# Rounded parts for two chunks of an output product, and a plain mean as the bias of the squares

## The chip, the cores and the metric

The kernel runs on one core of one Trainium2 chip. The metric is device time in microseconds, from launch to the last store. The engines of a core run at the same time and wait for each other on semaphores: TensorE (PE, with its weight loads as PEld), VectorE (DVE), ScalarE (ACT), GpSimd (POOL), and SyncE (SP), which issues the transfers.

## What is computed

One transformer block on 16 sequences of 1024 rows of 512 numbers, in float32: attention over 32 learned patterns with sparsemax in place of softmax, a residual and a normalization, then a small feed-forward part with a residual and a second normalization.

```python
A   = sparsemax((x @ Wq + bq).reshape(B, L, 16, 32) . keys / sqrt(32))
out = einsum('bhls,bshd->blhd', A, values)
out = transpose(out, (0, 2, 1, 3)).reshape(B, L, 512) @ Wo + bo
x   = layernorm(x + out)
s   = einsum('btd,dm->btm', x, Win) + bin_
h   = relu(s[..., None] * W1 + b1)
g   = einsum('btmh,mh->btm', h, W2) + b2
x   = layernorm(x + einsum('btm,md->btd', g, Wout) + bout)
```

The transpose ahead of the reshape mixes heads into rows, so that one row of `out @ Wo` belongs to one head and gathers 16 neighbouring rows of `A`. The kernel folds values and `Wo` into one matrix G for each head (512 by 512, four chunks of 128 rows). The "output product" of a tile is then four products of 128 by 128 probabilities with a 128 by 512 chunk of G.

## The kernel before, in words

The 16384 rows are 128 tiles of 128 rows. The order of the work is written out by hand as 151 slots. In slot n every engine does, for each step of the pipeline, that step for tile n minus the step's lag (the `LAG_` numbers): transposes of x in slot n for tile n, scores one slot later, the sparsemax steps up to lag 9 or 10, the output product at lag 23 (`LAG_WO`), the first normalization at lags 24 and 25, the feed-forward part at 26 to 34, the second normalization at 35 and 36. Each engine works through its own list in order, so an instruction that waits holds back all that is behind it on its engine.

**Start.** Slots 0 to 22 have no output product. In slots 5 to 20 the matrix G is made, one unit a slot (`pieces`, `piece`): a unit is four heads (index a) of one chunk c, so unit n has c = n mod 4 and lies in slot n + 5. PE multiplies (L891), ACT copies the four results from PSUM into four rows of a staging buffer, which are rows of `y_sb` (L1114), at the end of its slot, and SP stores them in four transfers to `G_of_heads` in DRAM (L454). There are two staging buffers, used in turn; the copies of a unit wait until the unit two slots before is stored. In the slots before 23 POOL also subtracts the step from the scores (L613), and in every slot up to 129 it folds two sums for the sparsemax (`fold`, L566), after ACT has written `side` and `above` (L1088, L1090). Within ACT's slot the order is: count (L1045), rounding of the transposed x (`xT_hi`, L1075, which waits for the score of the tile before, since there is one `xT_hi`), probabilities (L976, in two slots out of four), `side`, `above`, probabilities again, and then the copies of G.

**Output product.** SP loads the 1 MB of G of a head from DRAM for every tile (L467), into a ring of two. PE runs four float32 products (L856), each of which is issued as two matrix instructions. The scores of a tile are computed otherwise (`three_pass`, L749 to L751): each float32 operand is split into a rounded part and the rest, both of the type float32r, and hi times hi, hi times lo and lo times hi are added up, one instruction each.

**Normalization.** DVE adds the residual and sums the row (L1269). POOL makes two numbers of the sum, the mean scaled by the root of the row's length (L541) and the plain mean (L543). ACT squares with the first one as bias (L989). POOL makes the reciprocal root and the shift (L551, L556, L559), and ACT applies them (L1059, L1053). Every fourth slot ("split slot" below) has extra work: ACT and POOL add up and split the feed-forward sum (L1033, L1068, L1069 on ACT, L595 and L597 on POOL).

One tile of the first twelve needs a full sort on DVE, which takes DVE from 91 to 118 us.

Of the kernel before, what the change touches and what calls it, by code (L numbers as in the profile page):

```python
# [49 lines left out]
LAG_G = 22  # L50
# [14 lines left out]
def build_kernel(nc, query, key_param, Wq, bq, Wk, bk, Wv, bv, Wo, bo,  # L65
# [23 lines left out]
    with ExitStack() as ctx:  # L89
# [9 lines left out]
        GR, STAGES = 2, 2  # L99
# [26 lines left out]
        pT = sb("pT", [P, 2 * H * C * P])  # L126
        sum1 = sb("sum1", [P, 2])
        minus_mean1 = sb("minus_mean1", [P, 2])
        shift_sq1 = sb("shift_sq1", [P, 2])
# [13 lines left out]
        shift_sq2 = sb("shift_sq2", [P, 2])  # L143
# [8 lines left out]
        G_sb = sb("G_sb", [P, GR, C, D])  # L152
        V_rep, VT_rep = G_sb[:, 0].rearrange("p c n -> p (c n)"), G_sb[:, 1, 0, :]
        G_dram = nc.dram_tensor("G_of_heads", [H, P, C * D], F32, kind="Internal").ap()
# [18 lines left out]
        eps = sb("eps", [P, 1])  # L173
        per_row = sb("per_row", [P, 1])
        per_row_sq = sb("per_row_sq", [P, 1])
# [46 lines left out]
        s_Gst = [sem(f"s_Gst{r}") for r in range(STAGES)]  # L222
# [132 lines left out]
        def pair_place(turn, i):  # L355

            return (turn + i // UNROLL) % 2 * (H * C * P)
# [34 lines left out]

        def group_of(turn, i):

            return turn * (UNROLL // GROUP) + i // GROUP
# [3 lines left out]
        FILLS = 14 + S  # L399
# [3 lines left out]
        def _(sp):  # L403
# [35 lines left out]

            def slot(turn, j):  # L440
# [5 lines left out]
                for k in pieces(turn, j - 2):  # L446
                    heads, c, a = piece(k)
                    if a < HPC - 1:
                        continue
                    r = k // HPC % STAGES  # L450
                    sp.wait_ge(s_Gev, k + 1)
                    for n in range(HPC):
                        places = G_dram[HPC * heads + n].rearrange("(a s) n -> s a n", s=S)
                        sp.dma_start(places[:, :, c * D:(c + 1) * D],  # L454
                                     y_sb[n * S:(n + 1) * S, r * HPC:(r + 1) * HPC, :]).then_inc(s_Gst[r], 16)
                if in_range(turn, j, LAG_G):
                    i = j - LAG_G
                    h = i % H
                    if isinstance(turn, int) and base + i < H:
                        if h == 0:  # L460
                            sp.wait_ge(s_Gmm, PIECES)
                        if h % HPC == 0:
                            for r in range(STAGES):
                                sp.wait_ge(s_Gst[r], 16 * HPC * (h // HPC + 1) * (C // STAGES))
                    if not isinstance(turn, int) or base + i >= GR:
                        sp.wait_ge(s_o, base + i - GR + 1)
                    sp.dma_start(G_sb[:, i % GR].rearrange("p c n -> p (c n)"), G_dram[h]).then_inc(  # L467
                        s_G[i % GR], 16)
                if in_range(turn, j, LAG_XB):
                    i = j - LAG_XB  # L470
                    if base + i == 0:
                        for r in range(STAGES):
                            sp.wait_ge(s_Gst[r], 16 * (PIECES // STAGES))
# [32 lines left out]
        def _(pool):  # L506
# [15 lines left out]
            nc.gpsimd.memset(eps[:], EPS).then_inc(s_const, 1)  # L522
            nc.gpsimd.memset(per_row[:], -1.0 / D).then_inc(s_const, 1)
            nc.gpsimd.memset(per_row_sq[:], -1.0 / D ** 1.5).then_inc(s_const, 1)
# [11 lines left out]
            def mean(t0, par, s_rows, total, s_mean, minus_mean, shift_sq, s_shift):  # L536
# [9 lines left out]
            def norm(t0, par, s_var, var, s_ve, ve, s_mean, minus_mean, s_rstd, rstd, s_shift, shift, s_used):  # L546
# [4 lines left out]
                nc.gpsimd.tensor_tensor(ve[:], var[:, par:par + 1], eps[:], ALU.add).then_inc(s_ve, 1)  # L551
# [5 lines left out]
                pool.wait_ge(s_mean, 2 * t0)  # L557
# [11 lines left out]
            def slot(turn, j):  # L569
# [22 lines left out]
                if lead is not None and lead < ON_VECTOR:  # L592
# [6 lines left out]
                    pool.wait_ge(s_lo, lead // GROUP + 1)  # L599
                if in_range(turn, j, LAG_NORM1):  # L600
                    i = j - LAG_NORM1
                    mean(base + i + 1, i % 2, s_r1, sum1, s_mean1, minus_mean1, shift_sq1, s_shift1)
                if in_range(turn, j, LAG_NORM2):
                    i = j - LAG_NORM2
                    mean(base + i + 1, i % 2, s_r2, sum2, s_mean2, minus_mean2, shift_sq2, s_shift2)
# [9 lines left out]
                if in_range(turn, j, LAG_SIDE):  # L615
                    i = j - LAG_SIDE
                    fold(s_side, base + i + 1, side, s_foldc)
                    fold(s_above, base + i + 1, above, s_folds)

# [35 lines left out]
            mean(TILES, (TILES - 1) % 2, s_r1, sum1, s_mean1, minus_mean1, shift_sq1, s_shift1)  # L655
# [26 lines left out]
        def _(pe):  # L682
# [61 lines left out]
            def three_pass(ps, hi, lo, w_hi, w_lo, start, first):  # L744

                for c in range(C):
# [4 lines left out]
                    mm = nc.tensor.matmul(ps[:], lo[:, c, :], w_hi[:, c, :], start=False, stop=(c == C - 1))  # L751
                return mm
# [65 lines left out]
            def slot(turn, j):  # L818
# [26 lines left out]
                if in_range(turn, j, LAG_WO):  # L845
# [6 lines left out]
                    pe.wait_ge(s_G[i % GR], 16 * (turns_of(turn, j, LAG_WO, GR) + 1))  # L852
                    if not isinstance(turn, int) or base + i >= 2:
                        pe.wait_ge(s_r1, base + i - 1)
                    for c in range(C):
                        mm = nc.tensor.matmul(o_ps[i % 2][:],  # L856
                                              pT[:, bass.ds(pair_place(turn, i) + (i % H * C + c) * P, P)],
                                              G_sb[:, i % GR, c, :], start=(c == 0), stop=(c == C - 1))
                    mm.then_inc(s_o, 1)
# [22 lines left out]
                for k in pieces(turn, j):  # L882
# [3 lines left out]
                    if k >= HPC:  # L886
                        pe.wait_ge(s_Gev, k - HPC + 1)
# [655 lines left out]
```

## Time and profile before

| what | value |
|---|---|
| median of three runs | 1311.17 us (1311.08 to 1311.61) |
| profiled execution | 1313.41 us, of which span 1311.6 us |
| PE busy | 1248.0 us (95%) |
| DVE, ACT, POOL busy | 1133.2 us (86%), 1068.2 us (81%), 676.5 us (52%) |
| bytes moved by DMA | 258.35 MB, mean 197 GB/s |

The busy time is a mean over three stages: the start up to the first output product at 184 us, a long middle to 1141 us in which every slot holds all steps, and an end in which no scores are left. Matrix instructions are pipelined and overlap in the records, so the time that one takes is read from its start to the start of the next.

### The profile page before, as it was taken

The numbers are of one execution on the slowest core, as the hardware profiler recorded it, in microseconds if no ns is written. First come the engines' busy times: TensorE is split into PE (matmuls) and PEld (weight loads), VectorE is DVE, ScalarE is ACT, GpSimd is POOL, SyncE is SP. The second block draws the span as 40 slices with busy tenths as digits, with TensorE's granted clock in tenths as the row PEclk, the third lists the DMA queues.
The fourth block names the chain that finished last, engine by engine and source line by source line (L and its number), as shares of the span: only waits on it lengthen the run. The fifth ranks groups of instructions, "written<-read, shape, count | busy, mean of one in ns | idle before, by whom it ended". The sixth has DMA issues, their size and how long they took to land. (4 is left out here: it accounts for less than half of the span.)

```text
span 1311.6 us, 25223 instructions
## 1 busy us (share of the span) xinstructions
PE 1248.0 (95%) x5848; PEld 853.4 (65%) x5848; DVE 1133.2 (86%) x4538; ACT 1068.2 (81%) x2285; POOL 676.5 (52%) x1634
## 2 busy tenths in 40 slices
PE   8973899999999999999999999999999999989995
PEld 5642566676766767676776767677676767655552
DVE  3986899899999999999999999999999999966776
ACT  3661865779898888989898888989898888987776
POOL 1431333346555555655565555656555555665654
PEclk9995999999999999999999999999999999999998
DMA  6480785655656556565656656565655656468874
GB/s 203 131 215 17 199 246 192 191 185 171 218 184 216 198 197 206 190 217 182 220 188 208 203 191 214 185 220 183 213 196 199 211 186 216 162 227 281 280 233 104
DMA packets 92181, 258.35 MB, mean 197 GB/s; under 512 B 16067, under 2 KB 16067, under 8 KB 75622
## 3 DMA queue, kind: packets, MB, share of 16 engines
q1 hardware_dynamic: 91862, 256.26, 60.0%
q8 instruction: 48, 0.79, 0.3%
q14 instruction: 127, 1.04, 0.3%
q10 hardware_dynamic: 144, 0.26, 0.1%
HBM read 206.13 MB, written 50.33 MB: 196 GB/s over the span
## 5 line engine op out<-in xcount | busy, mean ns | idle before, releaser
L856 PE MATMUL bank<-G_sb,pT 128*128 128x512 f32 x1024 | 462.5, 594 | 2.8 <-DMA G_sb<-G_of_heads 2.1
L856 PEld LDWEIGHTS bank<-G_sb,pT 128*128 128x128 f32 x1024 | 185.2, 191 | 188.6 <-issue 184.3
L1426 DVE SCALAR_TENSOR_TENSOR acc<-hinge,w2c,acc 128x512 f32<-128x512 f32 x210 | 157.1, 748 | 81.7 <-ACT hinge L1019 80.2
L541 POOL TENSOR_TENSOR shift_sq<-sum,per_row_sq 128x1 f32<-128x1 f32 x244 | 95.2, 390 | 252.4 <-DVE y_sb L1269 250.5
L1376 DVE MAX8 top<-bank 128x8 f32<-128x32 f32 x2048 | 211.8, 178 | 0.0
L749 PE MATMUL bank<-A_hi,xT_hi 128*128 128x512 f32 x512 | 203.3, 397 | 0.0
L751 PE MATMUL bank<-A_hi,xT_lo 128*128 128x512 f32 x512 | 202.7, 396 | 0.0
L750 PE MATMUL bank<-A_lo,xT_hi 128*128 128x512 f32 x512 | 202.6, 396 | 0.0
L1019 ACT ACTIVATE hinge<-s_sb,b1c,w1c 128x512 f32<-128x512 f32 x240 | 192.8, 806 | 0.0
L1075 ACT CAST xT_hi<-bank 128x512 fp32r<-128x512 f32 x127 | 74.1, 584 | 134.8 <-PE bank L751 134.8
L989 ACT ACTIVATE unread<-y_sb,shift_sq 128x512 bf16<-128x512 f32 x244 | 174.5, 715 | 7.7 <-POOL minus_mean L543 7.5
L778 PEld LDWEIGHTS bank<-yT,Win_sb 128*128 128x128 f32 x1024 | 134.1, 191 | 62.7 <-issue 59.0
L556 POOL TENSOR_TENSOR rstd<-ve,minus_half 128x1 f32<-128x1 f32 x244 | 146.5, 600 | 41.1 <-POOL ve L551 40.7
L1269 DVE SCALAR_TENSOR_TENSOR y_sb<-bank,y_sb 128x512 f32<-128x512 f32 x244 | 160.4, 661 | 1.4 <-PE bank L802 0.7
L566 POOL TENSOR_TENSOR side<-side 128x256 bf16<-128x256 bf16 x128 | 86.5, 676 | 127.2 <-ACT side L1088 127.1
L778 PE MATMUL bank<-yT,Win_sb 128*128 128x128 f32 x1024 | 135.3, 275 | 0.5 <-ACT yT L1009 0.5
L751 PEld LDWEIGHTS bank<-A_hi,xT_lo 128*128 128x128 f32 x512 | 96.4, 188 | 23.9
L750 PEld LDWEIGHTS bank<-A_lo,xT_hi 128*128 128x128 f32 x512 | 96.4, 188 | 23.4
L813 PE MATMUL bank<-ident,u_sb 128*128 128x128 f32 x512 | 78.3, 276 | 33.5 <-DVEq L1389 26.2
L749 PEld LDWEIGHTS bank<-A_hi,xT_hi 128*128 128x128 f32 x512 | 97.1, 190 | 17.3
L1200 DVE TENSOR_TENSOR xT_lo<-bank,xT_hi 128x512 fp32r<-128x512 f32 x128 | 87.6, 684 | 22.6 <-ACT xT_hi L1075 22.3
L976 ACT ACTIVATE pT<-bank 128x512 f32<-128x512 f32 x128 | 76.4, 597 | 37.4 <-PE bank L813 35.6
(164 smaller groups left out, 2461.7 us busy)
## 6 DMA issues: line engine op xcount, KB each, us to landing
G_sb<-G_of_heads SPq DMA_DIRECT2D x128, 1024.0 KB, 5.5
x_sb<-in_L_attn_query_dram SPq DMA_DIRECT2D x128, 256.0 KB, 4.7
y_sb<-in_L_attn_query_dram SPq DMA_DIRECT2D x256, 128.0 KB, 5.4
out_dram<-o_sb SPq DMA_DIRECT2D x230, 128.0 KB, 4.7
G_of_heads<-y_sb SPq DMA_DIRECT2D x64, 256.0 KB, 4.0
out_dram<-y_sb SPq DMA_DIRECT2D x11, 256.0 KB, 3.3
y_sb<-in_L_attn_Wk_dram SPq DMA_DIRECT2D x1, 1024.0 KB, 5.9
y_sb<-in_L_attn_Wq_dram SPq DMA_DIRECT2D x1, 1024.0 KB, 8.1
```

Of the source, the lines that this page charges most:

```text
L541: nc.gpsimd.tensor_tensor(shift_sq[:, par:par + 1], total[:, par:par + 1], per_row_sq[:], ALU.mult).then_inc(s_mean, 1)
L556: nc.gpsimd.tensor_tensor(rstd[:, par:par + 1], ve[:], minus_half[:], ALU.pow).then_inc(s_rstd, 1)
L749: nc.tensor.matmul(ps[:], hi[:, c, :], w_hi[:, c, :], start=start and c == 0, stop=False)
L750: nc.tensor.matmul(ps[:], hi[:, c, :], w_lo[:, c, :], start=False, stop=False)
L751: mm = nc.tensor.matmul(ps[:], lo[:, c, :], w_hi[:, c, :], start=False, stop=(c == C - 1))
L778: mm = nc.tensor.matmul(s_ps[:, 0:P], Win_sb[:, c, :], yT[:, c, :], start=(c == 0), stop=(c == C - 1))
L856: mm = nc.tensor.matmul(o_ps[i % 2][:], pT[:, bass.ds(pair_place(turn, i) + (i % H * C + c) * P, P)], G_sb[:, i % GR, c, :], start=(c == 0 ...
L989: nc.scalar.activation(unread[:], y_sb[:, i % YR, :], ACT.Square, bias=shift_sq[:, i % 2:i % 2 + 1], scale=1.0 / D ** 0.5, accum_out=var[: ...
L1019: nc.scalar.activation(hinge[:, k % HR, :], s_sb[:, g % 2, :], ACT.Relu, bias=b1c[:, k:k + 1], scale=w1c[:, k:k + 1]).then_inc(s_hinge, 1)
L1269: nc.vector.scalar_tensor_tensor(rows, ps[:], 0.0, other, ALU.add, ALU.add, accum_out=total).then_inc(s_rows, 1)
L1376: mx = nc.vector.max(top8[:, h, :], z_ps[i % 2][:, h * S:(h + 1) * S])
L1426: nc.vector.scalar_tensor_tensor(acc[:], hinge[:, k % HR, :], w2c[:, k:k + 1], acc[:], ALU.mult, ALU.add).then_inc(s_acc, 1)
```

## The change

Of the four chunks of the output product, c = 0 and c = 2 stay float32. Chunks 1 and 3 are computed in three passes of rounded parts, as the scores are. For this:

- G is stored in DRAM and loaded as six blocks a head (`SPREAD`): two raw chunks, and a rounded one and a rest for each of the two others. A load moves 1.5 MB in place of 1 MB. The ring of G has three places in place of two, and a load is issued in the slot numbered i + 21 in place of i + 22.
- While G is made, ACT copies a result of chunk 1 or 3 twice, once as it is (`STAGE_LO`) and once rounded (`STAGE_HI`). POOL subtracts the rounded from the raw one in place, the first two heads one slot later and the last two heads two slots later, each time behind its folds. SP stores the rounded part two slots after the unit's slot and the rest three slots after it. There are three staging buffers (raw, rest, rounded); the copies of a unit of chunk 1 or 3 wait until the rounded part and the rest of the last such unit, two slots before, are stored.
- POOL splits the two chunks of probabilities of each tile (`part_hi`, `part_lo`: a copy and a subtraction of 128 by 256 numbers) one slot before the product, behind the norms and the split of the feed-forward sum and ahead of the means.
- The probabilities lie in 20 blocks that are passed from turn to turn, where there were two halves.
- The squares of both normalizations take the plain mean as bias, unscaled; the scaled mean (L541) is gone, and the step that adds epsilon also divides by the row's length.

The core of the diff:

```diff
-        GR, STAGES = 2, 2
+        GR, SETS = 3, 5
+        IN_PARTS, SPREAD = (1, 3), 6
...
+                for k in pieces(turn, j - 3)[HPC - 1:]:
+                    heads, c, a = piece(k)
+                    if in_parts(k):
+                        sp.wait_ge(s_Glo, parts_to(k))
+                        store_unit(heads, lo_col(c), STAGE_LO, s_Gst_lo)
...
-                nc.gpsimd.tensor_tensor(shift_sq[:, par:par + 1], total[:, par:par + 1], per_row_sq[:],
-                                        ALU.mult).then_inc(s_mean, 1)
...
+                if in_range(turn, j, LAG_PART):
+                    i = base + j - LAG_PART
+                    rows = p_blocks[:, parts_rows(i), i % HPC, :]
+                    pool.wait_ge(s_p, i // UNROLL * UNROLL + 3 * GROUP + i % H // HPC + 1)
+                    if i >= 2:
+                        pool.wait_ge(s_o, i - 1)
+                    nc.gpsimd.tensor_copy(part_hi[...], rows).then_inc(s_phi, 1)
+                    pool.wait_ge(s_phi, i + 1)
+                    nc.gpsimd.tensor_tensor(part_lo[...], rows, part_hi[...], ALU.subtract).then_inc(s_plo, 1)
...
                 if in_range(turn, j, LAG_SIDE):
                     fold(s_side, base + i + 1, side, s_foldc)
                     fold(s_above, base + i + 1, above, s_folds)
+                for k in [*pieces(turn, j - 2)[HPC // 2:], *pieces(turn, j - 1)[:HPC // 2]]:
+                    if in_parts(k):
+                        pool.wait_ge(s_Ghi, parts_to(k))
+                        nc.gpsimd.tensor_tensor(y_sb[:, STAGE_LO + a, :], y_sb[:, STAGE_LO + a, :],
+                                                y_sb[:, STAGE_HI + a, :], ALU.subtract).then_inc(s_Glo, 1)
...
+            def output_product(i):
+                for c in RAW:
+                    nc.tensor.matmul(o[:], p_blocks[...], G[:, raw_col(c), :].bitcast(F32), ...)
+                pe.wait_ge(s_plo, i + 1)
+                for n, c in enumerate(parts_of(i)):
+                    nc.tensor.matmul(o[:], hi, G[:, hi_col(c), :], start=False, stop=False)
+                    nc.tensor.matmul(o[:], hi, G[:, lo_col(c), :], start=False, stop=False)
+                    mm = nc.tensor.matmul(o[:], lo, G[:, hi_col(c), :], ...)
...
                 for k in pieces(turn, j):
                     act.wait_ge(s_Gmm, k + 1)
-                    nc.scalar.copy(y_sb[:, k % (HPC * STAGES), :], G_ps[k % HPC][:]).then_inc(s_Gev, 1)
+                    stored = 16 * HPC * (k // HPC // 2)
+                    if in_parts(k):
+                        if a == 0 and k >= 2 * HPC:
+                            act.wait_ge(s_Gst_hi, stored)
+                            act.wait_ge(s_Gst_lo, stored)
+                        nc.scalar.copy(y_sb[:, STAGE_LO + a, :], G_ps[a][:]).then_inc(s_Gev, 1)
+                        nc.scalar.copy(y_sb[:, STAGE_HI + a, :].bitcast(F32R), G_ps[a][:]).then_inc(s_Ghi, 1)
```

## Rows read from the trace of the kernel before

**Rows 1.** Busy time by stretch: us, PE, PEld, DVE, ACT, POOL, clock, DMA share, GB/s.
```profile
50.00:92.00 42.00, 37.93 (x204) 25.22 (x203) 36.20 (x188) 33.38 (x77) 16.67 (x21) 1.00 0.83 218
...
96.00:118.00 22.00, 0.00 (x0) 0.00 (x0) 17.14 (x160) 0.00 (x0) 0.00 (x0) 0.50 0.07 17
118.80:130.00 11.20, 10.43 (x31) 6.41 (x32) 7.97 (x35) 4.99 (x11) 3.40 (x4) 0.50 0.15 31
...
195.00:1141.00 946.00, 946.00 (x4472) 663.05 (x4471) 867.58 (x3437) 833.22 (x1783) 521.21 (x1237) 1.00 0.59 198
...
1193.00:1270.00 77.00, 74.91 (x313) 45.08 (x312) 55.92 (x121) 58.19 (x123) 46.50 (x143) 1.00 0.88 291
```

**Rows 2.** Timeline of ACT while G is made; in brackets idle time and its releaser.
```profile
120.03 0.60 ACT L976 ACTIVATE pT<-bank 128x512 f32<-128x512 f32 x1 [26.65 <-PE bank L813]
...
132.91 0.63 ACT L1090 ACTIVATE above<-u_raw 128x512 f32<-128x512 f32 x1
...
134.21 2.06 ACT L1114 COPY y_sb<-bank 128x512 f32<-128x512 f32 x4 [0.18 <-PE bank L891]
...
143.12 0.59 ACT L1075 CAST xT_hi<-bank 128x512 fp32r<-128x512 f32 x1 [0.93 <-PE bank L751]
...
144.23 0.62 ACT L1090 ACTIVATE above<-u_raw 128x512 f32<-128x512 f32 x1
144.75 2.04 ACT L1114 COPY y_sb<-bank 128x512 f32<-128x512 f32 x4
...
148.48 0.59 ACT L1075 CAST xT_hi<-bank 128x512 fp32r<-128x512 f32 x1 [1.07 <-PE bank L751]
```

**Rows 3.** Timeline of PE in one slot of the middle: start us, us, what.
```profile
607.45 0.60 PE L763 MATMUL bank<-ident,y_sb 128*128 128x128 f32 x4
...
608.32 3.60 PE L856 MATMUL bank<-G_sb,pT 128*128 128x512 f32 x8
611.76 1.05 PE L778 MATMUL bank<-yT,Win_sb 128*128 128x128 f32 x8
...
613.00 0.48 PE L801 MATMUL bank<-Wout_hi,split 128*128 128x512 f32 x1
613.32 0.39 PE L802 MATMUL bank<-Wout_lo,second 128*128 128x512 f32 x1
613.55 0.60 PE L692 MATMUL bank<-ident,x_sb 128*128 128x128 f32 x4
```

**Rows 4.** Instructions of the output product (L856) alone by stretch: PE, PEld, clock, DMA.
```profile
195.00:1141.00 946.00, 370.88 (x825) 148.53 (x824) 1.00 0.59 198
1193.00:1270.00 77.00, 50.89 (x112) 20.17 (x112) 1.00 0.88 291
```

**Rows 5.** Timeline of ACT and POOL around the split slot of the middle.
```profile
606.58 0.80 ACT L1059 ACTIVATE y_sb<-y_sb,shift,rstd 128x512 f32<-128x512 f32 x1
...
607.97 1.27 POOL L597 TENSOR_TENSOR split<-both,split 64x512 fp32r<-64x512 f32 x1 [1.38 <-ACT split L1068]
...
614.35 0.30 POOL L559 TENSOR_TENSOR shift<-minus_mean,rstd 128x1 f32<-128x1 f32 x1
...
617.00 0.19 POOL L541 TENSOR_TENSOR shift_sq<-sum,per_row_sq 128x1 f32<-128x1 f32 x1 [2.36 <-DVE y_sb L1269]
```

**Rows 6.** Groups of POOL's instructions by form: busy us, mean ns of one, idle before.
```profile
L566 POOL TENSOR_TENSOR above<-above 128x256 f32<-128x256 f32 x128 | 93.8, 733 | 0.0
...
L613 POOL TENSOR_TENSOR u_sb<-u_raw,step 128x512 f32<-128x512 f32 x20 | 21.0, 1048 | 94.3 <-DVE step L1340 94.3
```

**Rows 7.** Timeline of POOL, then of SP's queue, while G is made.
```profile
133.73 0.73 POOL L566 TENSOR_TENSOR above<-above 128x256 f32<-128x256 f32 x1
...
145.70 0.73 POOL L566 TENSOR_TENSOR above<-above 128x256 f32<-128x256 f32 x1
...
136.29 2.84 SPq L454 DMA_DIRECT2D G_of_heads<-y_sb  x4
```

**Rows 8.** DMA issues of the page: count, KB each, median us to landing.
```profile
G_of_heads<-y_sb SPq DMA_DIRECT2D x64, 256.0 KB, 4.0
```

More of the change, by code:

```diff
@@ L353, in so_far, with block_of, parts_of, parts_rows @@
             return min(max(n, 0), TILES) if isinstance(n, int) else n
-        def pair_place(turn, i):
-            return (turn + i // UNROLL) % 2 * (H * C * P)
+        blocks, spare = [{(n, c): n * C + c for n in range(C) for c in range(C)}], list(range(C * C, C * C + C))
+        for _ in range(1, TILES // UNROLL):
+            old = blocks[-1]
+            blocks.append({(n, c): old[c - 1, n] if c else spare[n] for n in range(C) for c in range(C)})
+            spare = [old[C - 1, c] for c in range(C)]
+        p_blocks = pT[:].rearrange("p (b a n) -> p b a n", a=HPC, n=P)
+        def block_of(i, c):
+            return blocks[i // UNROLL][i % H // HPC, c]
+        def parts_of(i):
+            return sorted(IN_PARTS, key=lambda c: block_of(i, c))
+        RAW = [c for c in range(C) if c not in IN_PARTS]
+        def parts_rows(i):
+            first, last = (block_of(i, c) for c in parts_of(i))
+            return slice(first, last + 1, last - first)
+        def raw_col(c):
+            return RAW.index(c)
+        def hi_col(c):
+            return len(RAW) + 2 * IN_PARTS.index(c)
+        def lo_col(c):
+            return hi_col(c) + 1
+        STAGE_RAW, STAGE_LO, STAGE_HI = 0, HPC, 2 * HPC
         def turns_of(turn, j, lag, ring):
@@ L391, in piece, with in_parts, parts_to @@
             return k // (HPC * C), k // HPC % C, k % HPC
+        def in_parts(k):
+            return piece(k)[1] in IN_PARTS
+        def parts_to(k):
+            return sum(in_parts(n) for n in range(k + 1))
         def group_of(turn, i):
@@ L438, in _, with store_unit @@
             AHEAD = 2
+            def store_unit(heads, col, stage, s_stored):
+                for n in range(HPC):
+                    places = G_dram[HPC * heads + n].rearrange("(a s) n -> s a n", s=S)
+                    sp.dma_start(places[:, :, col * D:(col + 1) * D],
+                                 y_sb[n * S:(n + 1) * S, stage:stage + HPC, :]).then_inc(s_stored, 16)
             def slot(turn, j):
@@ L445, in slot @@
                     sp.dma_start(x_sb[:, n % XR, :], x_tiles[n // UNROLL, n % UNROLL]).then_inc(s_x[n % XR], 16)
-                for k in pieces(turn, j - 2):
+                for k in pieces(turn, j - 2)[HPC - 1:]:
                     heads, c, a = piece(k)
[L448 to L455, printed above, removed]
+                    if in_parts(k):
+                        sp.wait_ge(s_Ghi, parts_to(k))
+                        store_unit(heads, hi_col(c), STAGE_HI, s_Gst_hi)
+                    else:
+                        sp.wait_ge(s_Gev, k + 1)
+                        store_unit(heads, raw_col(c), STAGE_RAW, s_Gst_raw)
@@ L462, in slot @@
                         if h % HPC == 0:
[L463 to L467, printed above, removed]
+                            units = h // HPC + 1
+                            sp.wait_ge(s_Gst_raw, 16 * HPC * len(RAW) * units)
@@ L851, in slot @@
                         pe.wait_ge(s_Gev, PIECES)
[L852 removed]
+                    pe.wait_ge(s_G[(base + i) % GR], 16 * ((base + i) // GR + 1))
                     if not isinstance(turn, int) or base + i >= 2:
                         pe.wait_ge(s_r1, base + i - 1)
[L855 to L859, printed above, removed]
+                    output_product(base + i).then_inc(s_o, 1)
                 if in_range(turn, j, LAG_YT):
@@ L1110, in slot @@
                 for k in pieces(turn, j):
+                    heads, c, a = piece(k)
                     act.wait_ge(s_Gmm, k + 1)
-                    if k % HPC == 0 and k >= HPC * STAGES:
-                        act.wait_ge(s_Gst[k // HPC % STAGES], 16 * HPC * (k // HPC // STAGES))
-                    nc.scalar.copy(y_sb[:, k % (HPC * STAGES), :], G_ps[k % HPC][:]).then_inc(s_Gev, 1)
+                    stored = 16 * HPC * (k // HPC // 2)
+                    if in_parts(k):
+                        if a == 0 and k >= 2 * HPC:
[3 more added lines that the diff above has]
+                        nc.scalar.copy(y_sb[:, STAGE_HI + a, :].bitcast(F32R), G_ps[a][:]).then_inc(s_Ghi, 1)
+                    else:
+                        if a == 0 and k >= 2 * HPC:
+                            act.wait_ge(s_Gst_raw, stored)
+                        nc.scalar.copy(y_sb[:, STAGE_RAW + a, :], G_ps[a][:]).then_inc(s_Gev, 1)
             slots(act, slot)
```

92 lines of the change are left out of this document (53 added, 39 removed).

## The prediction

> **What bounds the kernel now.** I read the busy time by stretch first, then a timeline of ACT while G is made, one of PE in the middle, and last POOL, SP's queue and the transfers. In the middle, from 195 to 1141 us, PE is busy for 946.00 us of 946.00, with DVE at 867.58 and ACT at 833.22 (92% and 88%) [rows 1]. So there every nanosecond taken from PE counts, until another engine's list becomes the longer one. The start is another stage: from 50 to 92 us PE is busy for 37.93 us of 42 and nobody is full [rows 1]. What paces it is a loop: ACT rounds the transposed x, DVE takes the rest, PE transposes the next tile and scores, and only then may ACT round again. The rounding of slot 16 starts at 143.12 and that of slot 17 at 148.48, 5.36 us apart, and ACT sat idle for 0.93 and 1.07 us ahead of them, waiting for PE [rows 2]. ACT can therefore be late by about 1 us a slot for nothing; all beyond it lengthens the slot. In the end, from 1193 to 1270 us, PE is busy for 74.91 us of 77 while DMA moves 291 GB/s at a share of 0.88 [rows 1].
>
> **Part 1, the product on PE.** A float32 product is two instructions; the eight of a tile start at 608.32 and what follows starts at 611.76, so a tile costs 3.44 us and one product 0.86. Float32r instructions of the same width stand in the same timeline: the second one takes 613.32 to 613.55, 0.23 us, and the first one behind float32 work 613.00 to 613.32, 0.32 us [rows 3]. The new product is 2 x 0.86 + 0.32 + 5 x 0.23 = 3.19, say 3.20 us, so 0.24 us a tile is saved. The middle holds 825 / 8 = 103 products, 9.18 us apart [rows 4]; with those of the last slots of the start, where PE has no gap either, I count 104: 25 us. From this comes what PE cannot use. In the split slot ACT ends y at 606.58 + 0.80 = 607.38 and PE transposes it at 607.45 [rows 3, 5]. PE would come 0.24 us sooner, and ACT's list in that slot has no gap, so up to 0.17 us of the gain is lost there. I take 0.2 us in every four tiles, 26 x 0.2 = 5 us, for this and for the split slot of part 2. The middle gives back 20 us.
>
> **Part 2, what POOL does in the middle.** The split of the probabilities is a copy and a subtraction of 128 by 256. The subtraction I take from the fold of that size, 0.73 us [rows 6]. Such a copy is not in the trace; it lies between nothing and the same 0.73, and I take 0.6, near the fold, as it reads one operand fewer. So 1.35 us a slot (0.73 to 1.46), against two small instructions of 0.19 us (L541) that go [rows 5]. In three slots of four POOL is idle for 2.36 us just before the means, behind the last shift, and the split hides there [rows 5]. In the split slot POOL comes out of L597 at 609.24 with no such gap [rows 5]: there the split delays the means, and ACT's first square a little. If that cover were gone in the other slots too, about 1 us a slot would end PE's gain. The new waits name things that are long done: the product waits for parts made a slot earlier, POOL for a product that its mean waits for anyway. The plain bias and the other epsilon keep engine and shape; I cost them at nothing, and at most one more small instruction of 0.19 us on POOL.
>
> **Part 3, making G, where I expect the loss.** Units of chunks 1 and 3 lie in every second slot: 6, 8, 10, ... 20. ACT's copies there are eight, not four. Four take 2.04 us, 0.48 each from start to start, so +1.9 us [rows 2], of which the idle 1 us hides half. The larger item is the wait ahead of them, for the rest of the unit two slots before. Follow it back: that rest is stored when POOL has subtracted the last two heads; POOL does so behind its folds of the *current* slot; these folds wait for ACT's `above` of the current slot, which stands right before the copies in ACT's list. So the wait cannot be met early, however fast the rest is made. Counted from the end of `above` it is:
>
> - to the end of the fold of `above`: 144.85 to 146.43 is 1.6 us in slot 16, 133.54 to 134.46 is 0.9 us in slot 14 [rows 2, 7];
> - two subtractions of 128 by 512 at the 1.05 us of L613 [rows 6]: 2.1 us (2.5 by the 1.27 of L597 [rows 5]);
> - four stores: issued within 2.84 us, so the last about 2.1 us after the first [rows 7], and 4.0 us to land [rows 8]: 6.1 us.
>
> That is 9.8 us in slots like 16 and 9.1 in slots like 14. Without it the copies start at 144.75, 0.1 us before the end of `above`, or at 134.21, 0.67 us behind it [rows 2]. The wait is thus 9.9 or 8.4 us. With 1.9 us of copies more and 1.0 us of idle time less, the slot grows by 10.8 us (slots 8, 16, 20) or 9.3 us (slots 10, 14, 18, which hold probabilities). Slot 6 has no wait, +0.9. Slot 12 has the wait, but DVE's sort runs beside it and ACT waits for 26.65 us up to 120.03 anyway [rows 2], so nothing is added. Sum: 3 x 10.8 + 3 x 9.3 + 0.9 = 61 us. What is late next is PE, which stands idle for most of each wait: the next unit's results need free PSUM banks, and the next score needs the next rounding. When PE stood still during the sort its granted clock was 0.50, and it was still 0.50 over 11.2 us of work afterwards [rows 1]. A score has 13 instructions at 0.23 us; at half clock that is 3 us more. I take 1.6 us, the middle of 0 and 3, for each of six waits: 10 us. The start loses 71 us. From below (subtractions at 0.73, 1 us less to land, no clock loss) it is 52; from above (1.27, 2 us more to land, all of the clock) 94.
>
> **Part 4, transfers.** G grows by half, 0.5 MB a tile. In the middle DMA moves 198 GB/s at a share of 0.59 [rows 1] with a product every 9.18 us; half a megabyte more is 57 GB/s, a share of 0.76, and the third place in the ring gives a slot more to land. I cost it at nothing there. In the end a product comes every 77 / 14 = 5.5 us [rows 4], and 291 GB/s have a share of 0.88 [rows 1]; at the same share per byte 331 GB/s is the most. A slot of the end would need 1.5 MB for G and 0.5 MB for rows in and out, 2.10 million bytes, or 6.3 us at 331: 0.8 us more over some 16 slots, +13 us. But that share counts packets that wait, too, three loads are at hand when the end begins, and PE asks 0.24 us less for 23 tiles, -5.5 us. I take 0, with -6 and +13 as bounds.
>
> On this the Trainium skill is stricter than my middle value: "SBUF — State Buffer", section "A bandwidth-pool intuition that's wrong", gives one core about 358 GB/s from HBM. By that figure a slot of the end would take 2.10 MB / 358 = 5.9 us, an estimate, and the sum would be some 6 us higher. No stretch shown here passes 291 GB/s, so the trace doesn't decide.
>
> **Sum.** The profiled execution took 1313.4 us, 1.8 of them outside its span of 1311.6. 1313.4 + 71 - 20 + 0 = 1364.4. It stands 2.2 us above the median of the runs, so for a median I predict 1362 us.
>
> **The rivals.**
>
> *The low part is off the path (faster).* If the wait of part 3 is met early, through an order of some queue that I misread, the start costs about 5 us for the longer copies, and the time is 1311 + 5 - 20 = 1296. For it: POOL is busy for only 16.67 us of 42 in the start [rows 1]. Against it: POOL's list ties the last two subtractions to folds of the same slot. It decides where each of six waits costs under 3.3 us (20 / 6). Chance 0.07.
>
> *The end is bound by transfers.* All of part 3 holds and the end costs the 13 us of part 4: 1375. For it speaks the share of 0.88, against it the longer ring. Chance 0.18.
>
> *POOL eats the gain of the middle.* The split outgrows the 2.36 us of idle time, or holds up DVE, so that y comes later by 0.24 us in every slot. Then the 20 us are gone: 1382. For it: DVE has only 8% left and POOL's list is in order. Against it: POOL is busy for 521.21 us of 946 [rows 1]. Chance 0.10.
>
> *The forecast*, 1362, has the remaining 0.65.
>
> **How the numbers follow.** Below, the start at 52 and the middle at its full 25: 1311 + 52 - 25 = 1338. Above, the start at 94 and the middle at 20, 1385, and 5 more for an end that is partly bound by transfers: 1390. This takes in both slow rivals and leaves out the fast one and corners, under 0.2 together. A difference under 0.2% (2.6 us) can't be told from none in this kernel. Only the fast rival ends on the other side; 0.01 of its 0.07 and 0.01 of the forecast's low corner I count as no change. Faster 0.06, same 0.02, slower 0.92.
>
> **What would show it.** In the new profile ACT's first copy in slots 8, 10, 14, 16, 18 and 20 should stand idle for 8 to 10 us until a store to `G_of_heads` lands; the granted clock should drop several times before 250 us; the first output product, at about 184 us before, should start at about 255. A product of the middle should take 3.20 us, products should be 9.0 us apart in place of 9.18, and PE should show small gaps ahead of the transposes of y in the split slot. The prediction is wrong if the first product starts before 200 us, or if the spacing in the middle does not fall.

## The result and the profile after

The changed kernel takes 1370.82 us (median of four runs, 1370.02 to 1371.21) against 1311.12 us for the kernel before on the same chip: a ratio of 1.0455, 95% interval 1.0437 to 1.0473. It is slower. The prediction was 1362 us with a range of 1338 to 1390.

I read the result by stage, with two marks on PE: the first output product, and the first one behind the last score (product 105). From start to start of these:

| stage | before, us | after, us | difference | predicted |
|---|---|---|---|---|
| start, to product 0 | 184.4 | 264.2 | +79.8 | +71 |
| middle, product 0 to 105 | 956.8 | 924.5 | -32.3 | -20 |
| end, product 105 to the end of the span | 170.4 | 180.7 | +10.3 | 0 |
| span | 1311.6 | 1369.4 | +57.8 | +51 |

The busy time by stretch, first in two windows of the start as in [rows 1], then the last part of the start, the middle and the end (PE, PEld, DVE, ACT, POOL, granted clock, DMA share, GB/s):

```profile
50.00:92.00 42.00, 28.14 (x120) 18.26 (x119) 26.08 (x112) 22.34 (x52) 18.44 (x19) 0.80 0.65 161
96.00:118.00 22.00, 14.66 (x52) 8.96 (x51) 10.52 (x39) 10.51 (x24) 8.19 (x9) 0.77 0.63 160
195.00:260.00 65.00, 37.35 (x145) 24.69 (x145) 32.54 (x133) 31.98 (x72) 25.53 (x27) 0.71 0.64 172
260.00:1141.00 881.00, 878.75 (x4496) 674.45 (x4497) 838.46 (x3331) 793.49 (x1709) 614.17 (x1193) 1.00 0.82 268
1258.00:1327.00 69.00, 58.17 (x272) 39.87 (x270) 44.41 (x94) 45.58 (x99) 44.05 (x117) 1.00 1.02 330
```

The start is emptier, not fuller: in 50 to 92 us PE has 120 matrix instructions where it had 204 [rows 1], no engine is busy for more than 28.14 us of 42, and the granted clock means 0.80. Of its two levels, 1.2 and 2.4 GHz, it is at the lower one for part of the time, and ahead of each fall PE had stood idle for part of the time. The middle is still PE's. In the end PE is no longer full, and DMA's share is above 1.

What empties the start is the first thing to look up. The waits from 30 to 260 us (who waited for whom, us in total, times, longest):

```profile
ACT y_sb L1195 <- DMA G_of_heads<-y_sb: 71.5, 7, 10.8
```

and one such wait in ACT's timeline:

```profile
65.14 0.61 ACT L1167 ACTIVATE above<-u_raw 128x512 f32<-128x512 f32 x1
76.56 0.59 ACT L1195 COPY y_sb<-bank 128x512 f32<-128x512 f32 x1 [10.80 <-DMA G_of_heads<-y_sb]
77.04 0.59 ACT L1196 CAST y_sb<-bank 128x512 fp32r<-128x512 f32 x1
...
79.91 0.67 ACT L1196 CAST y_sb<-bank 128x512 fp32r<-128x512 f32 x1
```

The wait ends with a store to `G_of_heads` and stands right behind `above`. POOL's timeline shows what made that store late:

```profile
66.78 0.74 POOL L615 TENSOR_TENSOR above<-above 128x256 f32<-128x256 f32 x1
67.47 2.65 POOL L684 TENSOR_TENSOR y_sb<-y_sb 128x512 fp32r<-128x512 f32 x2
```

From the end of `above` at 65.75 it is 1.72 us until the subtractions start behind its fold, 2.65 for the two of them, and 6.44 until the store has landed: 10.8 us.

A wait costs more than its length. The slot behind this one, slot 9, has no wait for a store, and yet it takes 11.00 us, from 81.01 to 92.01, where it took 7.41 before (from one rounding of the transposed x on ACT to the next). Its first part runs at the lower clock; two score instructions that follow each other then start 0.42 us apart where it is 0.23 at the higher level, and ACT waits 2.28 us for the score where it had waited 1.00. First the stretch, then PE, then ACT:

```profile
81.01:89.80 8.79, 7.59 (x23) 4.36 (x24) 6.07 (x26) 5.54 (x14) 5.02 (x5) 0.50 0.62 151
```
```profile
88.30 0.63 PE L816 MATMUL bank<-A_hi,xT_hi 128*128 128x512 f32 x1
...
88.72 0.63 PE L817 MATMUL bank<-A_lo,xT_hi 128*128 128x512 f32 x1
```
```profile
92.01 0.59 ACT L1152 CAST xT_hi<-bank 128x512 fp32r<-128x512 f32 x1 [2.28 <-PE bank L818]
```

In the middle, one product in PE's timeline, to be held against [rows 3] (the second group of three instructions is left out):

```profile
612.97 1.88 PE L825 MATMUL bank<-G_sb,pT 128*128 128x512 f32 x4
614.29 0.79 PE L830 MATMUL bank<-G_sb,part_hi 128*128 128x512 f32 x1
614.92 0.39 PE L831 MATMUL bank<-G_sb,part_hi 128*128 128x512 f32 x1
615.15 0.39 PE L832 MATMUL bank<-G_sb,part_lo 128*128 128x512 f32 x1
...
616.08 1.05 PE L859 MATMUL bank<-yT,Win_sb 128*128 128x128 f32 x8
```

It takes 616.08 - 612.97 = 3.11 us, 0.33 less than before, and no gap stands in it. Four products that follow each other came 9.13, 9.57, 9.13 and 8.98 us apart before and come 8.80, 9.23, 8.80 and 8.64 us apart now. Each slot gives back 0.33, the split slot too.

The waits of the end, 1258 to 1327 us:

```profile
PEld bank L825 <- DMA G_sb<-G_of_heads: 11.3, 10, 1.6
PE bank L825 <- DMA G_sb<-G_of_heads: 8.8, 9, 1.4
...
DVE y_sb L1355 <- DMA y_sb<-in_L_attn_query_dram: 7.9, 7, 1.8
```

PE waits for G at most tiles, which are 6.2 to 6.5 us apart; nearly all lay between 5.2 and 6.3 before.

### The profile page after: what moved, and what is told of

Same layout as the page of the kernel before. It is cut to its first block and busy times, and to the rows that moved or that the text cites. A ratio compares the mean times of both kernels' runs of the same rounds, so it can differ in the third digit from the quotient of the medians.

```text
span 1369.4 us, 25981 instructions
## 1 busy us (share of the span) xinstructions
PE 1238.4 (90%) x6104; PEld 917.0 (67%) x6104; DVE 1155.0 (84%) x4538; ACT 1078.6 (79%) x2317; POOL 851.5 (62%) x1676
## 3 DMA queue, kind: packets, MB, share of 16 engines
q14 instruction: 129, 1.05, 0.3%
## 5 line engine op out<-in xcount | busy, mean ns | idle before, releaser
L825 PE MATMUL bank<-G_sb,pT 128*128 128x512 f32 x512 | 244.5, 600 | 11.1 <-DMA G_sb<-G_of_heads 9.9
L605 POOL TENSOR_TENSOR rstd<-ve,minus_half 128x1 f32<-128x1 f32 x244 | 172.9, 709 | 43.0 <-POOL ve L600 42.7
L1066 ACT ACTIVATE unread<-y_sb,minus_mean 128x512 bf16<-128x512 f32 x244 | 174.5, 715 | 24.6 <-POOL minus_mean L592 23.6
L592 POOL TENSOR_TENSOR minus_mean<-sum,per_row 128x1 f32<-128x1 f32 x244 | 86.1, 359 | 133.9 <-DVE y_sb L1355 133.6
L830 PE MATMUL bank<-G_sb,part_hi 128*128 128x512 f32 x256 | 152.7, 596 | 0.0
L825 PEld LDWEIGHTS bank<-G_sb,pT 128*128 128x128 f32 x512 | 88.0, 192 | 75.8 <-issue 61.8
L1130 ACT ACTIVATE o_sb<-y_sb,shift,rstd 128x512 f32<-128x512 f32 x95 | 77.2, 813 | 44.8 <-POOL shift L608 44.7
```

Source lines behind the costliest of these rows:

```text
L605: nc.gpsimd.tensor_tensor(rstd[:, par:par + 1], ve[:], minus_half[:], ALU.pow).then_inc(s_rstd, 1)
L825: nc.tensor.matmul(o[:], p_blocks[:, block_of(i, c), i % HPC, :], G[:, raw_col(c), :].bitcast(F32), start=(c == RAW[0]), stop=False)
L830: nc.tensor.matmul(o[:], hi, G[:, hi_col(c), :], start=False, stop=False)
L1066: nc.scalar.activation(unread[:], y_sb[:, i % YR, :], ACT.Square, bias=minus_mean[:, i % 2:i % 2 + 1], scale=1.0, accum_out=var[:, i % 2:i ...
```

## The experiments

My theory: the start is lost to ACT's wait for the low part's store, which POOL's order makes late; the middle gains what PE saves; the end is bound by transfers. The rivals: the start is lost to the additional work itself; the middle's gain comes from the squares; the end is held by POOL. Each ratio below is against the kernel before on the same chip.

**Two places for the staging.** The rounded and the low part of units of chunks 1 and 3 go in turn to `y_sb` and to places that are free at that time:

```
+def lo_rows(k):
+    return y_sb[:, 4:8, :] if odd(k) else pT[:, C * C * HPC * P:].rearrange("p (a n) -> p a n", a=HPC)
+def hi_rows(k):
+    return y_sb[:, 8:12, :] if odd(k) else G_sb[:, 2, 0:HPC, :].bitcast(F32)
...
-if a == 0 and k >= 2 * HPC:
-    act.wait_ge(s_Gst_hi, stored)
-    act.wait_ge(s_Gst_lo, stored)
+if a == 0 and k >= 4 * HPC:
+    for s_stored in (s_Gst_hi[odd(k)], s_Gst_lo[odd(k)]):
+        act.wait_ge(s_stored, 16 * HPC * (k // HPC // 4))
```

> The changed kernel, but the rounded and the low part of a unit are staged in two places in turn, so that a unit's copies wait for the stores of the unit four slots before, not two; nothing else moves. Theory (the wait for the low part's store is the loss of the start): the waits of ACT ahead of its first copy, 7 x 10.2 us in the changed kernel, all go; what stays of the start's 79.8 us is the four additional copies in eight slots, some 6 to 9 us. The first product comes at 190 to 195 us in place of 264.2, the granted clock stays at full speed outside the sort, and the time is 1299 us (1293 to 1306). Rival (the start's loss is mostly the work itself: eight copies, POOL's subtractions, half again the stores, and the clock that falls with them): at least half of the 79.8 us stays, the time is 1330 us or more.

Measured: 1310.36 us, ratio 0.9981 (0.9968 to 0.9994). In its trace no wait of ACT for a store is left, and the first product comes at 199.5 us. So the wait is the loss of the start: 64.7 of 79.8 us went with it. 15.1 us stayed, not 6 to 9, and the middle and the end were each 2 us longer than in the changed kernel, so the time is 11 us above the theory's and outside its range.

**The last two subtractions first.** POOL makes them ahead of the step and the folds of their slot:

```
+for k in pieces(turn, j - 2)[HPC // 2:]:
+    ...
 if in_range(turn, j, LAG_STEP) and pool_steps(turn, j):
     ...
 if in_range(turn, j, LAG_SIDE):
     ...
-for k in [*pieces(turn, j - 2)[HPC // 2:], *pieces(turn, j - 1)[:HPC // 2]]:
+for k in pieces(turn, j - 1)[:HPC // 2]:
```

> The changed kernel, but POOL's last two subtractions of a unit stand ahead of the step and the two folds of their slot, not behind them. Theory (POOL's order ties the store to the current slot): the last subtraction ends 1.6 + 4 x 1.33 = 6.9 us after the above of the slot before, the store has landed 6.1 us later, and the copies are wanted some 6.4 us after that above; the wait falls from 10.2 to about 6.6 us, so 22 us are gained in six slots: 1349 us (1338 to 1354). Rival (the length of the store itself, or its queue, sets the wait): the wait stays at about 10 us and the time at 1371 us.

Measured: 1344.09 us, ratio 1.0243 (1.0224 to 1.0263). The wait fell to 5.6 us each, a little further than expected (one group of the waits from 30 to 240 us):

```profile
ACT y_sb L1201 <- DMA G_of_heads<-y_sb: 39.5, 7, 7.3
```

POOL's order does set the wait; the length of the store alone doesn't.

**The squares alone**, in the kernel before:

```
-bias=shift_sq[:, i % 2:i % 2 + 1], scale=1.0 / D ** 0.5,
+bias=minus_mean[:, i % 2:i % 2 + 1], scale=1.0,
```

> The kernel before with the second part of the change alone: the squares take the plain mean as bias at scale 1, and POOL makes one small number less for each. Theory (costed at nothing): no change, 1311 us within 1.5 us. Rival (the two small instructions that POOL no longer issues are the part of the middle's gain that I did not predict, 12 of 32 us): 1299 us, a spacing of 9.08 us in the middle.

Measured: 1312.55 us, ratio 0.9997 (0.9987 to 1.0008), with the spacing of the middle unchanged at 9.20 us. So the middle's gain does not come from it, and this half of the change costs and brings nothing that can be measured.

**Four of six blocks at the end:**

```
-sp.dma_start(G_sb[:, i % GR].bitcast(F32).rearrange("p c n -> p (c n)"), G_dram[h])
+some = 4 if i >= 105 else SPREAD
+sp.dma_start(G_sb[:, i % GR, 0:some].bitcast(F32).rearrange("p c n -> p (c n)"), G_dram[h, :, 0:some * D])
```

> The changed kernel, but from tile 105 on the load of G takes four of the six blocks, 1 MB as in the kernel before; PE makes the same passes and reads old data in the last two blocks (chunk 3 of the product is left wrong for these tiles). Theory (the end is bound by transfers): the products of the end are 5.2 to 5.5 us apart again, the stretch from product 105 to the end of the span falls from 180.7 to about 170 us, and the time is 1361 us (1358 to 1364). Rival (the end is longer for another reason: POOL's split, or the engines' order): the stretch stays at 180 us, the time at 1371 us.

Measured: 1365.79 us, ratio 1.0406 (1.0387 to 1.0426). The end took 173.1 us, 7.6 less; PE no longer waits for G, and DMA's share falls to 0.76:

```profile
1258.00:1327.00 69.00, 63.46 (x295) 45.88 (x295) 48.99 (x104) 50.00 (x108) 46.24 (x121) 0.95 0.76 247
```

Transfers are 7.6 of the 10.3 us, so the theory holds in the main, though the time is 2 us above its range. The size is not sharp: in the profiles of the kernels that load six blocks for every tile, this stretch takes 177.9 to 183.2 us. Three products of four then come 4.9 us apart, but the fourth, in the split slot, about 9.27. Three timelines of that slot, of ACT, DVE and POOL in this order:

```profile
1300.47 0.62 ACT L1111 COPY both<-acc 64x512 f32<-64x512 f32 x1 [0.57 <-DVE acc L1513]
1302.21 0.62 ACT L1146 CAST split<-both 64x512 fp32r<-64x512 f32 x1 [1.12 <-DVE both L1402]
...
1303.26 0.57 ACT L1087 COPY yT<-bank 128x512 f32<-128x512 f32 x1
```
```profile
1301.12 1.06 DVE L1402 TENSOR_TENSOR both<-acc,both 64x512 f32<-64x512 f32 x1
```
```profile
1300.90 0.74 POOL L659 TENSOR_TENSOR part_lo<-pT,part_hi 128x256 fp32r<-128x256 f32 x1
```

The copy of the transposed y stands behind ACT's `split` and `second`, and these wait for DVE's sum, which takes 1.06 us beside POOL's `part_lo`; in the kernel before it took 0.68 in every split slot of the end. That is 0.4 us of a slot that is 3 us longer than its like before. The rest of it I tried to find on POOL.

**The means first.** The same, with POOL's split of the probabilities behind the means of its slot:

```
-if in_range(turn, j, LAG_PART):
-    ...
 if in_range(turn, j, LAG_NORM1):
     ...
 if in_range(turn, j, LAG_NORM2):
     ...
+if in_range(turn, j, LAG_PART):
+    ...
```

> The run with four blocks loaded at the end (chunk 3 of the product left wrong from tile 105 on), and POOL's split of the probabilities moved behind the means of its slot, in all slots. Theory (at the end POOL's split stands ahead of the means, for which ACT's squares wait, and so lengthens a loop that PE's shorter slots have exposed): the products of a split slot come at most 6.3 us apart in place of 9.24, the others stay at 4.9, the stretch from product 105 to the end falls from 173.1 to 162 to 166 us, the time from 1366 to 1357 us (1354 to 1360). Rival (the split slot is held by the chain of the sums through ACT and DVE itself): the 9.24 stays, 1366 us.

Measured: 1378.02 us, ratio 1.0495 (1.0474 to 1.0516): 12 us slower. The theory of this run falls, and so does its rival. The split slots of the end do come down from 9.27 to 7.75 and 6.96 us, but other slots grow and the end stays at 174.1; and the middle takes 936.6 us, 12 more. There PE, which had no wait, now has one, 18 times in the waits from 300 to 1130 us:

```profile
PE bank L922 <- DVE differs L1379: 9.0, 18, 0.7
```

Why `differs` is late was not followed. In the same window ACT's waits for POOL's shift are 65.3 us in total, where they were 41.1 in the run before, so POOL's own list may be behind it.

**The means first with two places:**

> The run with two staging places (1310 us), and POOL's split of the probabilities behind the means of its slot; all six blocks of G are loaded. Theory (transfers bind the end, and POOL's order shows only where they don't): the products of the end stay 6.2 to 6.6 us apart, 1309 us (1306 to 1311). Rival (POOL's order costs its time beside the transfers as well): the end is 7 us shorter, 1303 us.

Measured: 1321.07 us, ratio 1.0067 (1.0046 to 1.0088), outside both. The middle lost 13 us, as in the run before; the end, at 178.9 us, is 4 shorter than with two places alone, which is within the 177.9 to 183.2 of like kernels. Its late products are still 6.4 to 7.2 us apart.

**No low part.** The subtractions cover 8 of 512 columns:

```
-nc.gpsimd.tensor_tensor(lo_rows(k)[:, a, :].bitcast(F32R), lo_rows(k)[:, a, :],
-                        hi_rows(k)[:, a, :], ALU.subtract).then_inc(s_Glo, 1)
+nc.gpsimd.tensor_tensor(lo_rows(k)[:, a, 0:8].bitcast(F32R), lo_rows(k)[:, a, 0:8],
+                        hi_rows(k)[:, a, 0:8], ALU.subtract).then_inc(s_Glo, 1)
```

> The run with two staging places (1310 us), with POOL's subtractions for the low part of G cut to 8 of 512 columns; waits, copies and stores stay as they are (most of the low part is left wrong). Theory (the 15 us that the start still loses are for the larger part POOL's: its 1.3-us subtractions stand ahead of the next step and folds, and DVE's operations take longer beside them): the first product comes at 189 to 193 us in place of 199.5, the time is 1302 us (1299 to 1305). Rival (the four additional copies of ACT in every second slot cost the 15 us): 199 us, 1310 us.

Measured: 1305.55 us, ratio 0.9938 (0.9920 to 0.9956), with runs from 1299.0 to 1312.1. The first product came at 195.7 us, between the two. That hides the size. Slots 8, 12, 16 and 20, from rounding to rounding, take 6.06 us each where they took 7.66, 7.71, 8.59 and 7.64: 7.4 us less. Of these, 3.2 are lost again in slot 9 (PE's clock was granted at 0.66 between 70 and 80 us), and behind the last slot of the start the first product waits 2.9 us for its load of G, which it did not do with two places.

**One chunk in parts**, the rest staged in two places in turn, and the means first:

```
-IN_PARTS, SPREAD = (1, 3), 6
+IN_PARTS, SPREAD = (1,), 5
```

> One chunk in parts in place of two, so that G has five blocks, 1.25 MB a tile; the other three are staged in two places in turn, as the whole was in the kernel before, and POOL's split of the probabilities stands behind the means. Theory (each loss scales with what is in parts, and no copy waits for a store): a product takes 6 x 0.43 + 3 x 0.23 = 3.27 us, so the middle gains 0.17 us a tile, 18 us; the start loses 4 to 8 us, the end at most 2: 1303 us (1298 to 1307), by this chip's time of the kernel before of 1311 to 1313. Rival (the losses at the start and the end don't shrink with the parts): 1310 us or more.

Measured: 1308.37 us, ratio 0.9968 (0.9953 to 0.9982). Product and middle behaved as worked out: 3.27 us in PE's timeline, and 939.8 us from product 0 to 105, 17.0 less than before. The end was 168.9 us, 1.5 *less*: at 1.25 MB a tile PE has no wait for G from 1196 to 1265 us, though DMA's share is 0.97 there. (POOL's split is half as large here and stands elsewhere, so this is not transfers alone.) But the start lost 13.5 us, hardly less than two chunks lose. So the start's rest doesn't scale with the parts in this run, and it is what keeps this version at 1308. 2.9 of it are slot 21, part of which ran at the lower clock.

**The subtractions after `cum`.** Why do 13 to 15 us stay? One slot of the run with two places, DVE and then POOL:

```profile
75.21 0.52 DVE L1496 TENSOR_TENSOR_SCAN cum<-go_on,top 128x128 f32<-128x128 f32 x1
75.77 1.20 DVE L1504 SCALAR_TENSOR_TENSOR cum<-cum,rank_inv 128x128 f32<-128x128 f32 x1
77.00 0.29 DVE L1510 TENSOR_REDUCE tau<-cum 128x16 f32<-128x128 f32 x1
```
```profile
75.40 2.72 POOL L699 TENSOR_TENSOR y_sb<-y_sb 128x512 fp32r<-128x512 f32 x2
```

The second operation on `cum` takes 1.20 us and ends at 76.97, just behind POOL's first subtraction (76.82). The same operation took 0.29 before. One line on POOL puts the subtractions elsewhere:

```
+pool.wait_ge(s_cand, base + j)
 pool.wait_ge(s_Ghi, parts_to(k))
 nc.gpsimd.tensor_tensor(lo_rows(k)[:, a, :].bitcast(F32R), lo_rows(k)[:, a, :],
                         hi_rows(k)[:, a, :], ALU.subtract).then_inc(s_Glo, 1)
```

> The run with two staging places (1310.4 us), and each of POOL's subtractions for the low part waits until DVE has made cum of the slot; all is computed. In that run DVE's two operations on cum take 0.52 to 1.34 and 1.2 us where a subtraction stands beside them, and 0.42 to 0.52 and 0.29 without one. Theory (an operation of DVE with two operands in SBUF stands still while POOL's subtraction runs, and that lengthens the slots of the start): both take 0.5 and 0.29 us again, the subtractions fall beside DVE's sums and the reading of PSUM; in six slots about 0.9 of 1.75 us come back, the first product at 193 to 196 us in place of 199.5, the time 1305 us (1302 to 1307). Rival (it is POOL's own list that is late: the subtractions hold up the next step and the folds, and start later now): the first product at 199 us or later, 1310 us or more.

Measured: 1303.52 us, ratio 0.9926 (0.9906 to 0.9946), the fastest version of this study, with everything computed. DVE's groups from 40 to 100 us, the run with two places and then this one (busy us, mean ns):

```profile
L1504 DVE SCALAR_TENSOR_TENSOR cum<-cum,rank_inv 128x128 f32<-128x128 f32 x8 | 6.9, 858 | 0.3
L1496 DVE TENSOR_TENSOR_SCAN cum<-go_on,top 128x128 f32<-128x128 f32 x8 | 5.8, 726 | 0.7 <-DVE top L1479 0.5
...
L1405 DVE TENSOR_SCALAR twice<-sum_side 128x16 f32<-128x16 f32 x9 | 1.5, 165 | 0.0
```
```profile
L1406 DVE TENSOR_SCALAR twice<-sum_side 128x16 f32<-128x16 f32 x9 | 5.0, 556 | 0.0
L1497 DVE TENSOR_TENSOR_SCAN cum<-go_on,top 128x128 f32<-128x128 f32 x8 | 3.9, 485 | 0.8 <-DVE top L1480 0.6
L1505 DVE SCALAR_TENSOR_TENSOR cum<-cum,rank_inv 128x128 f32<-128x128 f32 x8 | 2.3, 292 | 0.3
```

Both operations on `cum` are short again, and `twice` is now the one that stands still: 0.56 us in the mean for 0.165. The slots in which the delay showed, 8, 12, 16 and 20, became 6.17, 6.23, 6.17 and 6.03 us long, 7.0 us less than with two places (part of it is slot 16, which had run at the lower clock for 3.4 us there). In these four slots POOL subtracts the last two heads of chunk 1; those of chunk 3 fall into slots 10, 14 and 18, which took 7.33 us with two places and take 7.33 now. So one chunk had lost in the four slots nearly what two had: 8.2 us more than the kernel before, against 10.1. POOL's subtractions start later than before and these slots are still shorter, so POOL's own list is not what is late.

The first product came at 196.0 us, only 3.5 earlier, because now it waits for its load of G, which it did not do with two places:

```profile
196.01 3.26 PE L841 MATMUL bank<-G_sb,pT 128*128 128x512 f32 x4 [3.45 <-DMA G_sb<-G_of_heads]
```

The two profiled executions differ by 7.5 us: 3.5 in the start, -0.7 in the middle and 4.8 in the end, where the added line does nothing. So only half of what this version gains over two places is shown to come from the line.

> The run with one chunk in parts (1308.4 us) with the same wait for cum ahead of POOL's subtractions. Theory (DVE stands still beside them): half as many units, three or four slots with 0.9 to 1.75 us to win: the first product at 193 to 195 us in place of 197.9, 1305 us (1302 to 1307). Rival (POOL's list is late): 198 us or later, 1308 us or more.

Measured, the same line with one chunk: 1306.17 us, ratio 0.9948 (0.9933 to 0.9962). The first product came at 192.3 us, 5.6 earlier, with no such wait; slots 8, 12, 16 and 20 took 6.14 us each where they had taken 7.11, 7.11, 8.38 and 7.12. (The profiled execution is the fastest of five, 2.7 us under their median.) The theory holds a second time and the rival falls.

## Why the prediction was right, and where it was off

**Part 3, making G: right in mechanism, 9 us short.** Every link that I followed is in the trace: the folds of the current slot, two subtractions, the store, ACT idle. The slots of the start, from rounding to rounding on ACT, show where the time went (us more than in the kernel before):

| part of the start | changed kernel | two places | no low part | after `cum` |
|---|---|---|---|---|
| slot 6, without a wait | +0.8 | +0.8 | +0.8 | +0.8 |
| slots 8, 10, 14, 16, 18, 20 | +66.5 | +10.0 | +4.2 | +4.4 |
| the six slots right behind these | +13.7 | +1.1 | +2.7 | +3.6 |
| slots 12 and 13, with the sort | 0.0 | +2.6 | +1.4 | +0.1 |
| all else up to product 0 | -1.2 | +0.7 | +2.2 | +2.7 |
| product 0 | +79.8 | +15.1 | +11.3 | +11.6 |

Seven waits were found and six count: the one of slot 12 lies beside the sort and adds nothing, as predicted. The six are 60.9 us where I had 54.9; the terms that were small are the subtraction (1.33 us each for 1.05) and the store (6.44 from the end of the subtractions for 6.1). The longer copies take the other 5.6 of the 66.5 and 0.8 in slot 6, 6.4 for my 6.3. The clock I had at 10 us. The slots right behind the six waits lost 13.7; each of them ran in part at the lower clock and ended with ACT waiting for PE's score, so this is about what the clock cost. So the waits and the clock were each mis-sized, by 6 and by some 4 us.

What I left out is that POOL's subtractions hold up DVE's operations on `cum`. They do so in the changed kernel too (0.81 us in the mean for 0.29), but there the waits and PE's clock set the length of the slots, and nothing of it shows in the sum. It shows once the waits are gone: with two places it is about 7 of the 15.1 us, as both the run without the low part and the one with the subtractions after `cum` take that much out of slots 8, 12, 16 and 20. In the fastest version 11.6 us stay: about 5 for ACT's copies in the first two rows, 1.3 in slots 11 and 19, which may be `twice`, 2.1 in slot 21, which ran at the lower clock for 3.4 us, and 3.45 of waiting for the first load of G.

**Part 1: the product was mis-sized, 3.20 for 3.11 us.** 4 x 0.43 + 6 x 0.23 = 3.10: the first rounded pass behind float32 work costs nothing extra here, and I had charged 0.09. Over 105 tiles that is 9 us. The 5 us that I took off for the split slot did not come: its spacing falls by as much as the others. 105 x 0.33 = 34.7 is about the 32.3 seen; the first four slots of the stretch give back less. The run with one chunk repeats the sum for another mix, 3.27 worked out and 3.27 read.

**Part 2: the cover holds, by its place.** The copy takes 0.50 and the subtraction 0.76 us in the mean, 1.25 for my 1.35, and where the change put them, they hide. Behind the means they cost 12 to 13 us: PE then waits for DVE's `differs`, and what makes that late stays open. So the rival that POOL eats the gain of the middle was one move away, though it would have come by `differs`, and I had named y.

**Part 4: wrong for the end.** I took 0 and gave "the end is bound by transfers" 0.18; it is bound by them, at +10.3 of the +13 us. The step that failed is the discount: three loads at hand and the lower share. The 6.3 us a slot that I had as the bound is what the late slots took, 6.2 to 6.5 us at 330 GB/s and a share of 1.02. But the 331 GB/s behind it is not a ceiling: the changed kernel itself moved more just before that, and the run after `cum` more still (two stretches, one of each):

```profile
1231.00:1258.00 27.00, 25.11 (x126) 17.88 (x124) 19.06 (x40) 21.01 (x45) 16.63 (x44) 1.00 1.03 351
```
```profile
1182.00:1208.00 26.00, 24.65 (x122) 17.55 (x120) 19.08 (x41) 18.46 (x41) 17.88 (x48) 1.00 1.03 365
```

So that the bound met the number is in part luck, and what sets the rate at a full share stays open. The Trainium skill's 358 GB/s for one core ("SBUF — State Buffer", section "A bandwidth-pool intuition that's wrong") was not reached in the late slots, and was passed in the second of these stretches; the measurement decides. With 1 MB a tile 7.6 us came back, with 1.25 MB (and a smaller split on POOL) all of it. The last 2.7 us of the changed kernel's end stay open: the run that moved POOL's split did not win them.

**The rival that ended on the other side** needed each wait under 3.3 us. It had 0.07 and failed for the reason given against it. Once the wait is gone by another staging place, the change does end on that side, by less than 1%: 1310, and 1303.5 with the subtractions moved.

**The sum.** +71 - 20 + 0 stood against +79.8 - 32.3 + 10.3. The first and the third error together, 19 us, and the second, 12, have opposite signs, so the sum is 7 us low, and the forecast 9, with the 2 us that it took off for the median. That the total came nearer than its terms is luck.

## What to carry to other kernels

When work is added in the middle of a chain that reuses a buffer, count the whole round from the last read of the buffer back to its next write, over every queue in between, before looking at how busy the engines are; here 2.65 us of POOL work made 10 us of waits on an engine that was half idle, and a second buffer undid it. Price an idle gap of PE by the slot behind it as well: the six gaps cost 13.7 us in slots that had no wait. Read the time slot by slot and not by subtracting totals, since a delay that costs 7 us in one version hides in the waits of another. When a saving shortens one stage, look at which stage has the least room for what pays for it: half a megabyte a tile was free at a share of 0.59 and cost 8 to 10 us at 0.88. And work moved to an idle POOL is free only beside those operations of DVE that keep their time beside it: choose the place in POOL's list by what DVE does at that time.

## What the runs showed of the hardware

DVE's two operations on `cum`, which both have two operands in SBUF, stood still while a subtraction of 128 by 512 ran on POOL that had begun before them: 0.29 us became 1.20, and 0.42 to 0.52 became up to 1.34, each ending 0.15 to 0.28 us behind POOL's. The first one kept its 0.52 us where it had begun ahead of POOL's. Operations that read PSUM beside one operand in SBUF (`u_raw`, 0.69 us) or that reduce (`sum_side`, 0.41) kept their time. `twice`, with one operand in SBUF, stood still too, 0.165 to about 1.0. The Trainium skill says why such pairs meet: "SBUF — State Buffer", section "Who interferes with whom", has VectorE and GpSimd share one pair of ports, held for a whole instruction by the one that comes first. It counts instructions with two SBUF inputs among the cases, and `tensor_scalar` where it enters a two-port mode, and has `tensor_reduce` free of it on this chip. The traces here agree, as far as they show the lengths; which mode `twice` ran in no trace shows.
